# The residual add and the sum of squares of the second LayerNorm, emitted inside the output-projection loop instead of behind it

## What is computed

```python
q = (x @ Wq);  v = (x @ Wv)
state_t = lam * state_{t-1} + v_t          # per head, lam = sigmoid(beta)
y = LN(q * state) * ln_g + ln_b            # LN over D
y = y * silu(x @ Wg)
attn = y @ Wo                              # "output projection"
x2 = LN(x + attn)                          # second LayerNorm: the place of the change
h = silu(x2 @ Wgate) * (x2 @ Wup)
out = LN(x2 + h @ Wdown)
```

## Times and profile before

| what | us |
|---|---|
| timed runs: median of 2 (lowest, highest) | 2334.44 (2300.12, 2368.75) |
| the profiled execution, its own time | 2297.86 |
| its span on the slowest core (core 2) | 2296.2 |
| spans of the eight cores | 2284.3 to 2296.2 |
| busy on core 2: PE / DVE / ACT / POOL | 1907.1 / 578.2 / 343.1 / 110.3 |
| output projection, first to last matmul start (core 2) | 489.7 to 736.2 |
| first FFN matmul (core 2) | 839.53 |

### The profile page before, as it was taken

The page is one execution under the profiler, slowest core; times in us unless marked ns, Lnnn a source line. Parts: engine busy times, 40 slices in busy tenths (PEclk is TensorE's granted clock), DMA queues, the critical chain, the costliest instruction groups (busy, mean ns, idle before and its releaser), DMA issues.

```text
span 2296.2 us, 25245 instructions; the slowest of 8 cores (2284.3 to 2296.2 us)
## 1 busy us (share of the span) xinstructions
PE 1907.1 (83%) x9751; PEld 963.6 (42%) x9898; DVE 578.2 (25%) x1351; ACT 343.1 (15%) x402; POOL 110.3 (5%) x230
## 2 busy tenths in 40 slices
PE   4898999921878069999999999999999999998640
PEld 2346864300555034444444444444444444443220
DVE  4222234578313541100111111111111111111154
ACT  0100015300000202222112112112112111200002
POOL 1000000000000000000000000000000000000000
PEclk9999999955899569999999999999999999998875
DMA  8651343420041404446434434335434343421303
GB/s 121 118 92 35 59 67 69 72 68 1 1 74 24 123 11 81 74 74 110 74 73 88 77 56 92 74 57 102 81 61 86 74 75 73 90 39 37 70 4 146
DMA packets 32453, 161.04 MB, mean 70 GB/s; under 512 B 3668, under 2 KB 3668, under 8 KB 22100
## 3 DMA queue, kind: packets, MB, share of 16 engines
q0 software_dynamic: 29744, 142.62, 34.5%
q1 hardware_dynamic: 2596, 16.79, 2.0%
HBM read 293.62 MB, written 8.39 MB: 132 GB/s over the span
## 4 chain that ended last, share of the span: by engine, by line
PE 80%; DVE 10%; DMA 6%; issue 2%; ACT 2%; DVEq 0%; POOL 0%; ACTq 0%; POOLq 0%; SPq 0%
PE p L1044 19%; PE p L1075 19%; PE p L1138 19%; PE p L840 6%; PE p L492 5%; PE p L590 5%; PE p L370 4%; DMA warena<-wd_t 2%; DMA bbuf<-x_loc 2%; DMA warena<-wo 1%; DVE sqscr L790 1%; DVE sqscr L788 1%; DVE bbuf L797 1%; DMA sscr<-x_loc 1%; DVE sqscr L792 1%
## 5 line engine op out<-in xcount | busy, mean ns | idle before, releaser
L1044 PE MATMUL p<-tbuf,warena 128*128 128x512 bf16 x2006 | 462.6, 381 | 4.2 <-DVE tbuf L983 2.1
L1075 PE MATMUL p<-tbuf,warena 128*128 128x512 bf16 x2006 | 460.2, 379 | 2.2
L1062 ACT ACT_TABLE_LOAD x128 | 164.2, 1283 | 1010.2 <-PE p L1044 1010.2
L1044 PEld LDWEIGHTS p<-tbuf,warena 128*128 128x128 bf16 x2048 | 201.0, 98 | 245.3 <-issue 5.5
L1075 PEld LDWEIGHTS p<-tbuf,warena 128*128 128x128 bf16 x2048 | 200.4, 98 | 241.7
L1138 PE MATMUL p<-warena,vbuf 128*128 128x512 bf16 x1005 | 228.5, 387 | 34.6 <-DMA warena<-wd_t 32.5
L840 PE MATMUL p<-warena,bbuf 128*128 128x256 bf16 x1024 | 150.5, 283 | 99.6 <-DVE bbuf L797 43.6
L1138 PE MATMUL p<-warena,qbuf 128*128 128x512 bf16 x1004 | 221.1, 379 | 1.1
L1154 DVE TENSOR_TENSOR bbuf<-bbuf,p 128x512 bf16<-128x512 bf16 x128 | 88.0, 688 | 394.5 <-PE p L1138 394.5
L1138 PEld LDWEIGHTS p<-warena,vbuf 128*128 128x128 bf16 x1024 | 101.1, 99 | 161.3 <-issue 45.2
L840 PEld LDWEIGHTS p<-warena,bbuf 128*128 128x128 bf16 x1024 | 102.2, 100 | 149.2 <-issue 108.6
(11 more groups left out here) (125 smaller groups left out, 800.3 us busy)
## 6 DMA issues: line engine op xcount, KB each, us to landing
warena<-wgu_t POOLq DMA_DIRECT2D x128, 512.0 KB, 6.8
warena<-wd_t POOLq DMA_DIRECT2D x32, 1024.0 KB, 13.2
warena<-wq POOLq DMA_DIRECT2D x8, 1024.0 KB, 9.3
warena<-wv POOLq DMA_DIRECT2D x8, 1024.0 KB, 9.3
warena<-wg POOLq DMA_DIRECT2D x8, 1024.0 KB, 8.3
warena<-wo POOLq DMA_DIRECT2D x8, 1024.0 KB, 17.8
sscr<-x_loc SPq DMA_DIRECT2D x8, 1024.0 KB, 7.6
out_loc<-sscr SPq DMA_DIRECT2D x8, 1024.0 KB, 4.3
```

What stands on the lines that cost most here:

```text
L1044: inst = t.matmul(p[gbk][:, 0:NT], warena[:, (j % 2) * GUSL + k * OPW + ot * 128: (j % 2) * GUSL + k * OPW + (ot + 1) * 128], tbuf[:, k * ...
L1062: inst = sc.activation(sscr[:, SIL_OFF + (gg % 2) * NT: SIL_OFF + (gg % 2 + 1) * NT], p[gbk][:, 0:NT], AF.Silu)
L1075: inst = t.matmul(p[ubk][:, 0:NT], warena[:, (2 + j % 2) * GUSL + k * OPW + ot * 128: (2 + j % 2) * GUSL + k * OPW + (ot + 1) * 128], tbuf ...
```

## The change

A new function `emit_ln2A(ci)` holds the body of the residual loop, word for word: SP's load of x, DVE's residual add, DVE's sum of squares. The loop behind the output projection is gone; instead `emit_ln2A(ci)` is called inside the output projection's loop, right behind the cast of the last panel (pi = 7) of each chunk. The statistics loop and all that follows stay as they are.

```diff
@@ before the output projection
+    def emit_ln2A(ci):
+        xsl = (ci % 2) * D
+        mc = ci * 8
+
+        @blk.sync
+        def _(sy, ci=ci, xsl=xsl):
+            if ci < 2:
+                sy.wait_ge(sT, mil["l1bc_done"])
+            else:
+                sy.wait_ge(sV, mil[("l2res", ci - 2)])
+            mil[("xld", ci)] = dtick(sy.dma_start(
...
+        @blk.vector
+        def _(v, ci=ci, xsl=xsl, mc=mc):
+            dwait(v, mil[("xld", ci)])
+            v.wait_ge(sV, mil[("attn_ci", ci)])
...
@@ in the loop over half, ci and pl, behind the cast
                 ogrp += 1
+                if pi == NPAN - 1:
+                    emit_ln2A(ci)
     mil[("opdone", NPAN - 1)] = cnt["T"]
     mil["attn_done"] = cnt["V"]
-
-    for ci in range(NCH):
-        xsl = (ci % 2) * D
...
```

More of the change, by code:

```diff
@@ L804, in build_program, with _ @@
         bank_r[b] = ("V", mil["y2_done"])
+    def emit_ln2A(ci):
[8 more added lines that the diff above has]
+            mil[("xld", ci)] = dtick(sy.dma_start(
+                AP(sscr, xsl, [[SFREE, 128], [1, D]]),
+                AP(x_loc.tensor, ci * 128 * D, [[D, 128], [1, D]])),
+                "xld%d" % (ci % 2))
+        @blk.vector
+        def _(v, ci=ci, xsl=xsl, mc=mc):
+            dwait(v, mil[("xld", ci)])
+            v.wait_ge(sV, mil[("attn_ci", ci)])
+            rsl = qbuf[:, ci * D:(ci + 1) * D]
+            inst = v.scalar_tensor_tensor(rsl, rsl, 1.0, sscr[:, xsl:xsl + D],
+                                          ALU.mult, ALU.add,
+                                          accum_out=mscr[:, mc:mc + 1])
+            mil[("l2res", ci)] = tick(inst, "V")
+        @blk.vector
+        def _(v, ci=ci, mc=mc):
+            v.wait_ge(sV, cnt["V"])
+            rsl = qbuf[:, ci * D:(ci + 1) * D]
+            inst = v.scalar_tensor_tensor(sqscr[:, 0:D], rsl, 1.0, rsl,
+                                          ALU.mult, ALU.mult,
+                                          accum_out=mscr[:, mc + 1:mc + 2])
+            mil[("l2sq", ci)] = tick(inst, "V")
     wo_banks = [4, 5, 6]
```

## The result

The changed kernel takes 2267.54 us (median of nine runs) against 2303.24 us for the kernel before (eight runs). The ratio of the two is 0.9851, with a 95% interval of 0.9839 to 0.9864: 1.5% faster, 34.3 us (2267.54 / 0.9851 = 2301.8 for the kernel before).

A forecast was written before the change was run, and what follows sets the result against it. PE sets the pace, but idles in one 69.2 us wait while DVE runs residual pairs, statistics and normalize. From 2297.86 us, chain -39.7 with stalls, loads and clock at 0 gives 2258.2 us; range 2247 to 2274.

The forecast's parts named there:

- One pair off the chain is 4.61 us, seven are won, and the waits of 7.1 us with them: 39.7 us: Between last projection cast and statistics: the 44.32 us residual part shrinks to one 4.61 us pair, saving 39.7 us.
- PE's waits in the projection 0, with 0.8 us to spare: Output projection: a pair delays two casts, but free PSUM banks cover PE with 0.8 us to spare; cost 0.
- the start of the pair at 0.34: Output projection: the pair was taken to start 0.34 us after the panel-7 cast's start and end at 4.95.
- The x loads find their place, no wait: Output projection: each reload of x has 14.6 us to land beside idle DMA engines, so the 7.1 us wait is gone.
- Clock 0: Before the FFN: PE still starts at half clock after a 29.5 us pause, same price give or take 2 us.
- The sum: Whole kernel: chain -39.7, PE stalls 0, loads 0, clock 0, from 2297.86 us to 2258.2 us.
- the other cores gain a little less: Other cores: core 4 gains 36.5 us at the residual adds, but ends 12 us earlier anyway.
- Half clock in the projection: Output projection: held-back casts make PE pause and drop to half clock, costing 34 us, 2292 us; chance 3%.
- Late loads: Output projection: x loads land late and DVE's 7.1 us waits return ahead of casts, 7 us, 2265 us; chance 5%.
- Slower through loads: Output projection: very slow x loads block DVE's casts and stop PE; 2319 us at 35 us per load; chance 2%.
- No gain: Behind the pairs: something else sets the chain, so the change does less; 2298 us at full failure; chance 2%.
- Clock kept at full through the shorter pause: Before the FFN: a shorter PE pause keeps full clock, giving back 5.6 us in all, near 2252 us; chance 4%.

The follow-up runs named there:

- the two kernels without open loads: Kernel before and changed kernel, each with last-window down-projection weights loaded one block ahead; ratios 0.9816 and 0.9644 to the kernel before.
- sq_twice: Changed kernel with the sum of squares done twice in each pair, the second into an unused column; ratio 0.9906, runs 2280.3 to 2284.5 us.
- oneslot: Changed kernel with one slot for x instead of two, each load issued after the previous chunk's residual add; ratio 0.9811, runs 2261.1 and 2266.1 us.

## Why the prediction was right, and where it was off

- *One pair off the chain is 4.61 us, seven are won, and the waits of 7.1 us with them: 39.7 us.* Right. 38.2 us on the mean of eight cores, 39.5 on core 0, 36.3 on core 4 (by the same sum 36.5 were predicted); 39.8 us between the slowest cores of the two kernels without open loads, 37.7 on their means.
- *PE's waits in the projection 0, with 0.8 us to spare.* The zero was right to about 1 us, the margin was not: sq_twice showed 0.4 us. The step that fell short was the start of the pair at 0.34 (0.53 measured, as the add waits for the cast beside it) and the missing time from the cast's end to PE's start (0.25). The 0 stood on what was left; what a pair gets longer beyond 0.4 us is paid seven times.
- *The x loads find their place, no wait.* Right, shown by the missing row and by oneslot, which needed not even the second slot.
- *Clock 0.* Right: the first FFN group took 5.21 us to the next start (799.29 to 804.50), within the 4.87 to 5.81 of before.
- *The sum.* This is the step that failed, by its size: it had no term for anything behind the first FFN matmul. The tail gave back 6.0 us on the mean in the profiled executions; between the kernels with and without open loads it is 3.4 us on the mean core (37.7 - 34.3) and 5.5 on the slowest (39.8 - 34.3). Of the 9.3 us between 2258.2 and 2267.5 the gain that fell short is 5.4 (39.7 - 34.3); the other 3.9 us are that I started from the profiled run at 2297.86, while the kernel before lies at 2301.8 by the ratio. I had said that the other cores gain a little less but end earlier anyway; the unequal gain was in view, and I did not ask what it did to the distance between cores.
- *The rivals.* Half clock in the projection: did not happen, and even with real stalls cost some 2 us and not 34 (sq_twice). Its price was also off by its own row: 3.54 - 2.16 is 1.4 us per group and not 1.2, 39 us for 28 groups. Late loads: did not happen. Slower through loads: excluded by oneslot. No gain: excluded. Clock kept at full through the shorter pause: no; the stretch from 740 us shows 0.50 in the changed kernel as well:

```profile
740.00:760.00 20.00, 0.00 (x0) 0.00 (x0) 6.70 (x42) 9.98 (x13) 0.00 (x0) 0.50 0.62 100
```

In sq_twice, with PE pausing at every fourth group, the granted clock was 0.91 to 0.92 in two stretches and the cost some 2 of 15.8 us. The Trainium skill ("TensorE: Matmul & The Clock Gate", A second HAM failure mode) says that short pauses in a rotation through PSUM banks can make the clock go to and fro; the trace of sq_twice agrees, with pieces at 0.50 and an estimated price of some 2 us.

## What to carry to other kernels

Work of another engine that waits at the end of a PE stage only because of the order in which it was written can go between that engine's casts, as long as each piece is shorter than what the PSUM banks cover. Count that cover from start to start, begin the piece only where the step that it needs is done, and add the time from the end of the late cast to PE's start (0.25 us here), for the margin is small and every piece pays for it. Then look for the places where several cores load with nothing beside it: the gain of 37.7 us was 34.3 with three open loads behind it, and by the pattern above this goes with how far apart neighbouring cores are. And when a chain is left over with rounds of tiny instructions across two engines, make one round of them: eight columns cost hardly more than one there (3.2 against 2.9 us).

## What was not expected of the hardware

- Loads that two neighbouring cores issue near the same time: with one pair of cores 1.4 us apart the tail with three open loads of 2 x 1024 KB took 166 us, with four pairs 6.5 to 8.6 us apart 155 to 157 us, and without open loads 116.5 us. That the distance is the cause is not shown.
- PE's time behind an open load is more than the wait: 31.4 us of waits made the tail 39.4 us longer, and 8 matmuls behind a wait took 3.57 us where 16 take 3.62 elsewhere.
- A set of statistics on 128x8 took 3.2 us, one on 128x1 2.9 us.
- A DMA of 1024 KB through SP's queue landed in 4.7 to 5.3 us in quiet (oneslot), and in up to 14.0 us beside four loads of 512 KB from POOL's queue.
- An add on DVE that needs the cast just before it started 0.11 us after that cast's end, and PE started 0.25 us after the end of the cast that it waited for.
